# Backward loops of a gated delta-rule layer: one half's decay moves from VectorE's three-plane product to ScalarE and GpSimd

## The chip, the cores and the metric

The kernel runs on one core of a Trainium2 chip. The metric is the device time of one execution in microseconds (us), inputs in device memory to outputs in device memory. Before the change three runs took 650.96, 650.63 and 649.58 us; the median is 650.63 us.

## The reference

The model is one layer over x of shape (4, 1024, 128): a layer norm, a linear attention with a recurrent state, a residual, a second layer norm, and a mixture of 16 experts with a shared expert, again with a residual. The loops that the change touches belong to the attention. With 16 heads of width 8 its state S is an 8x8 matrix for each head and batch, and one step is

```
bs1 = einsum('bhk,bhkv->bhv', kt, S);   S1 = S + at[..., :, None] * bs1[..., None, :]
S2  = exp(gft)[..., None] * S1
bs2 = einsum('bhk,bhkv->bhv', kt, S2)
S3  = S2 + at[..., :, None] * bs2[..., None, :] + kt[..., :, None] * vt[..., None, :]
o   = einsum('bhk,bhkv->bhv', qt, S3)
out3 = stack([z, z, o], axis=2).reshape(B, 3 * N, H, HD);   out = out3[:, -N:]
```

Only the last third of the steps reaches the output, but their state depends on all 1024 steps.

## The kernel before

The 1024 tokens of each batch are cut into 32 chunks, which lie side by side in the 128 columns (4 batches x 32 chunks) while the 128 partitions hold heads and key rows. The first region of each chunk has L1 = 21 positions, the second L2 = 11, so there are NT = 32 positions. Since a step is linear in S, every chunk's whole effect can be computed before its start state is known. That is done by the backward loops: they start at the last position of a region, carry for each chunk an 8x8 matrix (rows that are multiplied into the steps from the left), and take 32 steps, 21 for the first region and 11 for the second. Later the chunks are chained (65 small products in series), then 11 forward steps run from the true start states, and the experts' part runs beside and behind them.

In the backward loops the carried state has 128 x 1024 values, in two halves of 512 columns, half 1 and half 0. Half h lies in PSUM bank 2h. Step n (n = 0 to 31 in all that follows, numbered by the `u_term` with which VectorE begins it) does for each half:

- `u_term` (L1490, VectorE): multiplies the sums over a head's rows, which TensorE left in bank 2h+1, by the factors PP, into SBUF.
- `y_term` (L1496, VectorE): multiplies the sums in bank 2h by the keys K, in place.
- `add_u_term` (L1091, GpSimd): adds the u term to the decayed state (`decayed`, which is plane 0 of `grown`).
- `move_on` (L1502, VectorE): adds `decayed` to bank 2h, which gives the next state, in the same bank.
- `grow` (L1468, VectorE): multiplies the new state by three planes of factors in one instruction, FF (the decay), Y and K. Planes 1 and 2 (`work`) feed TensorE, plane 0 is `decayed`. It is issued by `step`, for half 1 before the `move_on` of half 0, and for half 0 behind it.
- `sums` (L1878 and L1879, TensorE): two products with a block matrix over `work`, two passes each, into banks 2h+1 and 2h.
- beside this, ScalarE copies bank 2h+1 to SBUF (L883), GpSimd multiplies the copy by the values V (`v_times_u`, L1008), and TensorE adds the result to a running sum (`add_sum`, L1888).

Every engine works through its own queue in the order in which the code was written; semaphores hold an instruction until what it needs is there. Nothing reorders them. Between these steps lies the front work of later positions, four positions to a group: a table (`uses`) says at which step TensorE transposes and projects the group, ScalarE evicts the projections from PSUM (L733, L740, L746), and VectorE (`keys` L1405, `c_keys` L1412, `rk_of` L1396) and GpSimd (`gate_keys` L1047, `y_of` L1054, `y_keys` L1063, `p_of` L1069) finish its factors. The group for step n+3 gets its keys, values and queries at steps 2, 6, 10, 14, 18 and 22, its gates and decays one step later. PSUM banks 6 and 7 are handed round for all this (`port`, `taken`): TensorE waits for the eviction of a bank before it fills it again.

## Time and profile before

| | |
|---|---|
| median of three runs | 650.63 us (649.58 to 650.96) |
| the profiled execution | 648.87 us, its span 647.1 us |
| PE busy | 516.5 us, 80% |
| VectorE (DVE) busy | 489.2 us, 76% |
| GpSimd (POOL) busy | 363.1 us, 56% |
| ScalarE (ACT) busy | 257.0 us, 40% |
| backward loops | from 24 us to 308 us |

The profile lists what each engine did and when. The chain that ended last follows the end of the program back through whatever released each instruction. In it "issue" is time in which an engine waited for nothing visible. In the rows of the time line the first number is the start and the second the duration, both in us; a bracket at a row's end is the idle time of the engine before it and what ended that. PE rows are matrix products, and their ends are modelled. The shares of busy time are averages over very different stages; only the backward loops matter here.

### The profile page before, as it was taken

What the parts mean: (1) busy time and instruction counts of PE and PEld (TensorE: products, weight loads), DVE (VectorE), ACT (ScalarE), POOL (GpSimd) and SP (SyncE); (2) the same over time, 40 slices, a digit from 0 to 9 for tenths busy, and PEclk for the clock granted to TensorE, in tenths of its full rate; (3) what the DMA queues carried; (4) which work ended last, traced back from release to release, by engine and by line L of the source; (5) the groups of instructions that cost most, each with busy time, mean ns of one, the idle gap of its engine ahead of it and who ended that gap; (6) DMA issues with size and microseconds to landing.
All of it is one profiled execution on the core that took longest, in us unless ns stands there. A gap on an engine that the chain in (4) does not pass through costs nothing.

```text
span 647.1 us, 7400 instructions
## 1 busy us (share of the span) xinstructions
PE 516.5 (80%) x1809; PEld 269.2 (42%) x1810; DVE 489.2 (76%) x787; ACT 257.0 (40%) x542; POOL 363.1 (56%) x353
## 2 busy tenths in 40 slices
PE   3889899999999885777776889789999956398830
PEld 2543434444444332322444455434443353355520
DVE  5697999989898998999799997788999656322201
ACT  4477543444444432112442345524554115044510
POOL 2378776757576564764786343567766574600033
PEclk9999999999999999988999899989999968889985
DMA  7701138400000691000711133101100011112134
GB/s 179 191 18 32 33 89 217 113 1 1 1 1 1 171 344 38 1 0 0 187 43 41 42 97 73 50 9 32 32 16 9 13 54 32 53 50 65 57 85 114
DMA packets 46946, 41.79 MB, mean 65 GB/s; under 512 B 4700, under 2 KB 40360, under 8 KB 46536
## 3 DMA queue, kind: packets, MB, share of 16 engines
q1 hardware_dynamic: 43332, 35.61, 20.2%
q0 software_dynamic: 2448, 5.38, 3.0%
q10 hardware_dynamic: 1136, 0.46, 0.3%
q8 instruction: 12, 0.20, 0.1%
q14 instruction: 18, 0.15, 0.1%
HBM read 23.80 MB, written 17.63 MB: 64 GB/s over the span
## 4 chain that ended last, share of the span: by engine, by line
PE 35%; DVE 29%; issue 14%; POOL 12%; DMA 4%; ACT 3%; SPq 0%; POOLq 0%; DVEq 0%; ACTq 0%
PE ps L1925 10%; DVE grown L1468 9%; PE ps L1942 5%; POOL grown L1091 4%; DVE ps L1502 4%; PE ps L1878 3%; PE ps L1932 2%; DVE early L1569 2%; DVE grown L1490 2%; PE ps L1982 2%; PE ps L1683 2%; POOL uv L1008 2%; PE ps L1879 2%; POOL early L1037 2%; PE ps L1983 2%
## 5 line engine op out<-in xcount | busy, mean ns | idle before, releaser
L1091 POOL TENSOR_TENSOR grown<-grown 128x512 f32<-128x512 f32 x64 | 80.5, 1267 | 91.6 <-DVE grown L1490 91.6
L1468 DVE TENSOR_TENSOR grown<-ps,steps 128x1536 f32<-128x1536 f32 x64 | 112.1, 1752 | 1.6
L1878 PE MATMUL ps<-grown,cst 128*128 128x512 f32 x128 | 72.7, 650 | 25.3 <-DVE grown L1468 24.7
L883 ACT ACTIVATE uv<-ps 128x512 f32<-128x512 f32 x64 | 38.1, 597 | 104.8 <-DVE grown L1490 104.8
L1925 PE MATMUL ps<-steps 128*128 x128 | 68.8, 635 | 8.4 <-issue 8.2
L1008 POOL TENSOR_TENSOR uv<-uv,steps 128x512 f32<-128x512 f32 x64 | 67.4, 1075 | 1.9 <-ACT uv L883 1.9
L1879 PE MATMUL ps<-grown,cst 128*128 128x512 f32 x128 | 67.1, 606 | 0.0
L1360 DVE TENSOR_TENSOR e_h<-rk,ps 128x256 f32<-128x256 f32 x64 | 25.4, 418 | 53.4 <-ACT rk L900 34.6
L1888 PE MATMUL ps<-uv,cst 128*128 128x512 f32 x128 | 60.4, 594 | 0.6 <-POOL uv L1008 0.6
L1167 POOL TENSOR_TENSOR early<-state,qT 128x512 f32 x22 | 37.1, 1688 | 34.0 <-DVE state L1482 34.0
L1490 DVE TENSOR_TENSOR grown<-ps,steps 128x512 f32<-128x512 f32 x64 | 43.3, 676 | 7.4 <-PE ps L1878 7.4
L1502 DVE TENSOR_TENSOR ps<-ps,grown 128x512 f32<-128x512 f32 x60 | 41.6, 693 | 9.4 <-POOL grown L1091 9.4
L1037 POOL DMA_INDIRECT early<-ys_mixed,slots_mixed x11 | 10.5, 956 | 64.7 <-DMA ys_mixed<-e_y 61.7
L1496 DVE TENSOR_TENSOR ps<-ps,steps 128x512 f32<-128x512 f32 x64 | 44.1, 689 | 1.1 <-PE ps L1879 1.0
L1878 PEld LDWEIGHTS ps<-grown,cst 128*128 128x128 f32 x128 | 21.0, 196 | 57.2 <-DVE grown L1468 51.2
L1138 POOL COPY early<-early 128x32 f32<-128x32 f32 x63 | 27.2, 434 | 28.1 <-DVE early L1574 28.0
L1569 DVE TENSOR_TENSOR early<-early 128x256 f32<-128x256 f32 x63 | 40.1, 636 | 1.3
L900 ACT ACTIVATE rk<-ps 128x256 f32<-128x256 f32 x64 | 23.9, 383 | 39.9 <-PE ps L1925 38.2
L1879 PEld LDWEIGHTS ps<-grown,cst 128*128 128x128 f32 x128 | 25.2, 197 | 32.2 <-issue 32.2
L1942 PE MATMUL ps<-steps,e_hT 128*128 x256 | 35.9, 284 | 2.8 <-ACT e_hT L904 2.7
L1888 PEld LDWEIGHTS ps<-uv,cst 128*128 128x128 f32 x128 | 24.2, 190 | 31.8 <-issue 29.6
L1942 PEld LDWEIGHTS ps<-steps,e_hT 128*128 128x128 f32 x256 | 31.5, 191 | 9.1 <-issue 8.0
(228 smaller groups left out, 1008.0 us busy)
## 6 DMA issues: line engine op xcount, KB each, us to landing
steps<-gate_up_proj SPq DMA_DIRECT2D x1, 4096.0 KB, 16.7
xs_others<-zeros SPq DMA_DIRECT2D x1, 2496.0 KB, 11.0
steps<-xs_others SPq DMA_DIRECT2D x19, 128.0 KB, 2.2
ys_others<-e_y SPq DMA_DIRECT2D x19, 128.0 KB, 1.8
early<-chain_m SPq DMA_DIRECT2D x4, 512.0 KB, 6.3
xf<-x SPq DMA_DIRECT2D x4, 495.0 KB
normed<-early SPq DMA_DIRECT2D x28, 64.0 KB, 1.7
xs_mixed<-zeros SPq DMA_DIRECT2D x1, 1728.0 KB, 8.9
```

Source lines behind the costliest of these rows:

```text
L1008: return G.tensor_tensor(wide(dst, w), wide(src, w), per_col(tile, k, 1, h, w), ALU.mult)
L1091: G.tensor_tensor(decayed[:, h], decayed[:, h], work[:, h, 1], ALU.add).then_inc(s_add[h], 1)
L1468: V.tensor_tensor(grown[:, :, h].rearrange("p e (x w) -> p e x w", w=HD), st, per_col(tile, FF, 3, h, HD), ALU.mult).then_inc(s_prod[h], 1)
L1490: V.tensor_tensor(wide(work[:, h, 1], HD), wide(ps[h][:, 1], HD), per_col(tile_of(i), PP, 1, h, HD), ALU.mult).then_inc(s_uterm[h], 1)
L1496: V.tensor_tensor(wide(bank[2 * h], HD), wide(bank[2 * h], HD), per_col(tile_of(i), K, 1, h, HD), ALU.mult).then_inc(s_term[h], 1)
L1502: V.tensor_tensor(dst, bank[2 * h], decayed[:, h], ALU.add).then_inc(s_state[h], 1)
L1569: V.tensor_tensor(ch_pr[:, m % 2, :, :, 0:HD], ch_m[r][:, :, i, :].rearrange("p j i -> p i j").unsqueeze(1) .to_broadcast([P, 4, HD, HD]), ...
L1878: T.matmul(bank[2 * h + 1], c["block"], work[:, h, 1], start=True, stop=True).then_inc(s_usum[h], 1)
L1879: T.matmul(bank[2 * h], c["minus"], work[:, h, 0], start=True, stop=True).then_inc(s_red[h], 1)
L1888: T.matmul(bank[4 + h], c["ident"], vterm[:, h], start=i in (0, L1), stop=i + 1 in (L1, NT)).then_inc(s_ba[h], 1)
L1925: T.matmul(b_gu(run, b)[u], e_xT[:, b, u], gu[:, bass.ds(ex * (2 * F), 2 * F)], start=True, stop=True).then_inc(s_eg, 1)
L1942: ins = T.matmul(b_y(run)[:, u * D:(u + 1) * D], e_hT[:, u, f * P:(f + 1) * P], dw[:, bass.ds(ex[u] * F + f * D, D)], start=(f == 0), stop ...
```

## The change

In half 1 the decay plane leaves VectorE's product. `grow(1, ...)` now writes two planes (Y and K, 128x1024), while `grow(0, ...)` still writes three. ScalarE copies bank 2, the state of half 1, to a new SBUF buffer `rows_copy`, behind its two `uv` copies and ahead of its front work, and GpSimd multiplies this copy by FF into `decayed` in a new `decay_rows`, behind the u term's addition of half 0. Two semaphores are new. `s_rc` says that the copy is made; both GpSimd and the VectorE's `grow(1)` wait for it, the latter since TensorE may overwrite bank 2 once `grow` has ended. `s_rd` says that GpSimd has made the product; the next copy and the next addition wait for it. At step 0 the state is a constant and no copy is made: `decay_rows(0)` reads the constant.

```diff
             for i in range(NT):
 ...
                     S.activation(ucopy[:, h], bank[2 * h + 1], ACT.Copy).then_inc(s_uc[h], 1)
+                if i + 1 < NT:
+                    act.wait_ge(s_state[1], i + 2 + (i + 1 >= L1))
+                    act.wait_ge(s_rd, i + 1)
+                    S.activation(rcopy[:], bank[2], ACT.Copy).then_inc(s_rc, 1)
                 front(i)
...
+            def decay_rows(step):
+
+                if step:
+                    pool.wait_ge(s_rc, step)
+                rows = (rcopy[:].rearrange("p (e x w) -> p e x w", e=1, w=HD) if step else
+                        c["diag8"].unsqueeze(1).unsqueeze(1).to_broadcast([P, 1, P // 2, HD]))
+                G.tensor_tensor(wide(decayed[:, 1], HD), rows, per_col(tile_of(step), FF, 1, 1, HD), ALU.mult
+                                ).then_inc(s_rd, 1)
+
+            decay_rows(0)
             for i in range(1, NT + 1):
                 coming = NEED.index(i + 2) if i + 2 in NEED[2:] else None
+                pool.wait_ge(s_rd, i)
                 add_u_term(1, i - 1)
...
                 add_u_term(0, i - 1)
+                if i < NT:
+                    decay_rows(i)
                 if coming is not None:
                     y_of(coming)
...
-            def grow(h, tile, ready):
+            def grow(h, tile, ready, copied):
 
+                lo = 1 if h else 0
                 dve.wait_ge(s_state[h], ready)
-                st = bank[2 * h].unsqueeze(1).to_broadcast([P, 3, HALF]).rearrange("p e (x w) -> p e x w", w=HD)
-                V.tensor_tensor(grown[:, :, h].rearrange("p e (x w) -> p e x w", w=HD), st, per_col(tile, FF, 3, h, HD),
-                                ALU.mult).then_inc(s_prod[h], 1)
+                if h and copied:
+                    dve.wait_ge(s_rc, copied)
+                st = bank[2 * h].unsqueeze(1).to_broadcast([P, 3 - lo, HALF]).rearrange("p e (x w) -> p e x w", w=HD)
+                V.tensor_tensor(grown[:, lo:, h].rearrange("p e (x w) -> p e x w", w=HD), st,
+                                per_col(tile, FF + lo, 3 - lo, h, HD), ALU.mult).then_inc(s_prod[h], 1)
```

ScalarE's queue at step 6, where it evicts keys and values of a group (L740 and L746; after the change L742 and L748). First as it was, with the two `uv` copies ahead:

```order
L883 ACTIVATE uv<-ps 128x512 [waits s_bp1,s_uterm1]
L883 ACTIVATE uv<-ps 128x512 [waits s_bp0,s_uterm0]
L740 ACT_TABLE_LOAD
L740 ACTIVATE steps<-ps 128x4x128 [waits s_filled7]
L746 ACTIVATE steps<-steps 128x4x128 [waits s_taken7]
```

The same place in ScalarE's queue after the change:

```order
L885 ACTIVATE uv<-ps 128x512 [waits s_bp1,s_uterm1]
L885 ACTIVATE uv<-ps 128x512 [waits s_bp0,s_uterm0]
L889 ACTIVATE rows_copy<-ps 128x512 [waits s_rows_decayed,s_state1]
L742 ACT_TABLE_LOAD
L742 ACTIVATE steps<-ps 128x4x128 [waits s_filled7]
L748 ACTIVATE steps<-steps 128x4x128 [waits s_taken7]
```

The table load and all evictions of the step now stand behind a copy that waits for half 1's next state.

GpSimd's queue at the same step 6 and the start of step 7, before the change (L1091 the additions, L1047, L1054 and L1063 the group's factors, L1008 the products with V):

```order
L1091 TENSOR_TENSOR grown<-grown 128x512 [waits s_uterm1]
L1047 TENSOR_TENSOR steps<-steps 128x4x128 [waits s_taken6]
L1091 TENSOR_TENSOR grown<-grown 128x512 [waits s_uterm0]
L1054 TENSOR_TENSOR steps<-steps 128x4x128 [waits s_taken7,s_gk]
L1008 TENSOR_TENSOR uv<-uv,steps 128x512 [waits s_ba1,s_uc1]
L1008 TENSOR_TENSOR uv<-uv,steps 128x512 [waits s_ba0,s_uc0]
L1063 TENSOR_TENSOR e_y<-steps 128x512 [waits s_filled6,s_y]
L1091 TENSOR_TENSOR grown<-grown 128x512 [waits s_uterm1]
```

And after it:

```order
L1097 TENSOR_TENSOR grown<-grown 128x512 [waits s_uterm1,s_rows_decayed]
L1053 TENSOR_TENSOR steps<-steps 128x4x128 [waits s_taken6]
L1097 TENSOR_TENSOR grown<-grown 128x512 [waits s_uterm0]
L1105 TENSOR_TENSOR grown<-rows_copy,steps 128x512 [waits s_rows_copied]
L1060 TENSOR_TENSOR steps<-steps 128x4x128 [waits s_taken7,s_gk]
L1014 TENSOR_TENSOR uv<-uv,steps 128x512 [waits s_ba1,s_uc1]
L1014 TENSOR_TENSOR uv<-uv,steps 128x512 [waits s_ba0,s_uc0]
L1069 TENSOR_TENSOR e_y<-steps 128x512 [waits s_filled6,s_y]
L1097 TENSOR_TENSOR grown<-grown 128x512 [waits s_uterm1,s_rows_decayed]
```

One product (L1105) is new, and everything behind it up to the next step's addition is one product later in the queue.

VectorE's queue from the `y_term` of half 0 to the `grow` of half 0, before:

```order
L1496 TENSOR_TENSOR ps<-ps,steps 128x512 [waits s_red0]
L1468 TENSOR_TENSOR grown<-ps,steps 128x3x512 [waits s_state1]
L1502 TENSOR_TENSOR ps<-ps,grown 128x512 [waits s_add0,s_term0]
L1468 TENSOR_TENSOR grown<-ps,steps 128x3x512 [waits s_state0]
L1405 TENSOR_TENSOR steps<-steps,ps 128x4x128 [waits s_filled6]
```

And after:

```order
L1518 TENSOR_TENSOR ps<-ps,steps 128x512 [waits s_red0]
L1490 TENSOR_TENSOR grown<-ps,steps 128x2x512 [waits s_rows_copied,s_state1]
L1524 TENSOR_TENSOR ps<-ps,grown 128x512 [waits s_add0,s_term0]
L1490 TENSOR_TENSOR grown<-ps,steps 128x3x512 [waits s_state0]
L1424 TENSOR_TENSOR steps<-steps,ps 128x4x128 [waits s_filled6]
```

The order is the same. Half 1's `grow` has one plane less and one wait more.

## Rows read from the trace of the kernel before

**Rows 1.** The page's costliest groups: busy us, mean ns, idle before and its releaser.

```profile
L1468 DVE TENSOR_TENSOR grown<-ps,steps 128x1536 f32<-128x1536 f32 x64 | 112.1, 1752 | 1.6
...
L883 ACT ACTIVATE uv<-ps 128x512 f32<-128x512 f32 x64 | 38.1, 597 | 104.8 <-DVE grown L1490 104.8
```

**Rows 2.** Windows of steps 5 and 6: length, then busy PE, PEld, DVE, ACT, POOL.

```profile
76.27:84.21 7.94, 6.92 (x25) 3.54 (x24) 7.65 (x11) 3.48 (x7) 4.56 (x4) 1.00 0.08 20
84.21:91.61 7.40, 6.94 (x16) 2.58 (x14) 7.11 (x9) 4.19 (x6) 6.64 (x6) 1.00 0.33 84
```

**Rows 3.** Time line of step 6 (start us, duration us, engine, line).

```profile
84.21 0.68 DVE L1490 TENSOR_TENSOR grown<-ps,steps 128x512 f32<-128x512 f32 x1
...
84.93 0.60 ACT L883 ACTIVATE uv<-ps 128x512 f32<-128x512 f32 x1 [3.29 <-DVE grown L1490]
84.97 1.27 POOL L1091 TENSOR_TENSOR grown<-grown 128x512 f32<-128x512 f32 x1 [3.44 <-DVE grown L1490]
...
86.34 0.70 DVE L1502 TENSOR_TENSOR ps<-ps,grown 128x512 f32<-128x512 f32 x1 [0.25 <-POOL grown L1091]
...
87.55 1.75 DVE L1468 TENSOR_TENSOR grown<-ps,steps 128x1536 f32<-128x1536 f32 x1
...
89.88 2.10 POOL L1008 TENSOR_TENSOR uv<-uv,steps 128x512 f32<-128x512 f32 x2
```

**Rows 4.** A two-plane product of the forward steps, queried by its line.

```profile
L1461 DVE TENSOR_TENSOR grown<-state,steps x22: 1224/1226/2122, 406.0 to 500.6; 128x1024 f32<-128x1024 f32 x22
```

**Rows 5.** Time line of step 7 (91.61 to 100.40).

```profile
93.17 2.49 POOL L1091 TENSOR_TENSOR grown<-grown 128x512 f32<-128x512 f32 x2
...
94.53 0.70 DVE L1502 TENSOR_TENSOR ps<-ps,grown 128x512 f32<-128x512 f32 x1 [0.93 <-POOL grown L1091]
```

**Rows 6.** Time line of step 14 (150.74 to 158.79).

```profile
153.26 1.28 ACT L740 ACT_TABLE_LOAD   x1
...
154.88 0.60 ACT L740 ACTIVATE steps<-ps 128x512 f32<-128x512 f32 x1 [0.33 <-PE ps L1683]
...
156.77 1.04 PE L1746 MATMUL ps<-wT,wnat 128*128 128x16 f32 x8
157.65 1.10 PE L1878 MATMUL ps<-grown,cst 128*128 128x512 f32 x2
```

**Rows 7.** Time line of step 3 (58.10 to 68.11): evictions, and TensorE behind them.

```profile
62.24 0.70 DVE L1502 TENSOR_TENSOR ps<-ps,grown 128x512 f32<-128x512 f32 x1 [2.15 <-POOL grown L1091]
...
62.83 0.60 ACT L740 ACTIVATE steps<-ps 128x512 f32<-128x512 f32 x1 [0.81 <-PE ps L1683]
63.54 0.30 PEld L1705 LDWEIGHTS ps<-e_y,cst 128*128 128x128 f32 x2 [0.72 <-issue]
...
64.82 0.23 PE L1714 MATMUL ps<-cst,wnat 16*128 16x16 f32 x1
```

**Rows 8.** Time line of step 1 (41.11 to 50.69): an eviction, and its end.

```profile
45.16 0.60 ACT L740 ACTIVATE steps<-ps 128x512 f32<-128x512 f32 x1 [0.29 <-PE ps L1683]
...
50.01 0.31 ACT L717 ACTIVATE rstd<-mv,eps 128x11 f32<-128x11 f32 x1
50.34 0.23 DVE L1375 RECIPROCAL rstd<-rstd 128x11 f32<-128x11 f32 x1 [1.21 <-ACT rstd L717]
```

**Rows 9.** Time line of step 21, the first of the second region.

```profile
215.85 1.75 DVE L1468 TENSOR_TENSOR grown<-ps,steps 128x1536 f32<-128x1536 f32 x1
...
216.67 1.08 ACT L883 ACTIVATE uv<-ps 128x512 f32<-128x512 f32 x2
```

**Rows 10.** Time line of step 22: a table load and what follows.

```profile
223.80 1.28 ACT L740 ACT_TABLE_LOAD   x1
225.09 0.49 ACT L740 ACTIVATE steps<-ps 128x384 f32<-128x384 f32 x1
```

**Rows 11.** The chain at the end of the loops: start us, us, what.

```profile
307.23 0.70 DVE state L1502
307.95 2.91 DMA chain_m<-state
```

More of the change, by code:

```diff
@@ L287, in build @@
         s_usum, s_uterm = two("s_usum"), two("s_uterm")
+        s_rc, s_rd = sem("s_rows_copied"), sem("s_rows_decayed")
         s_bc = sem("s_bcopy")
@@ L375, in build @@
         e_h, e_hT = sb("e_h", [P, U, F]), sb("e_hT", [P, U, F])
+        rcopy = sb("rows_copy", [P, HALF])
         xnT = [e_h[:].rearrange("p u f -> p (u f)"), e_hT[:].rearrange("p u f -> p (u f)")]
@@ L1519, in step @@
                     dve.wait_ge(s_yk, NEED.index(i) + 1)
-                grow(h, tile_of(i), i + 1 + (i >= L1))
+                grow(h, tile_of(i), i + 1 + (i >= L1), i)
             step(1, 0)
```

## The prediction

> **What bounds the kernel now.** I first read the chain that ended last. Its end of the backward loops shows the last `move_on` and, 0.02 us behind it, the transfer of the result [rows 11]. So the loops lie on the path, and whatever they gain or lose goes one to one into the total. Then the costliest groups: the three-plane `grow` is VectorE's largest there, 1752 ns, 64 times, with only 1.6 us idle before all of them [rows 1]. The windows of single steps say who sets the pace. In step 5 VectorE is busy for 7.65 of 7.94 us and GpSimd for 4.56. In step 6, where GpSimd also makes a group's factors, VectorE has 7.11 of 7.40 us and GpSimd already 6.64 [rows 2]. VectorE bounds, but GpSimd has 3.4 us to spare in the one and 0.8 us in the other, and the change adds a product of about 1.05 us to each. Last I read single steps on the time line, to see where ScalarE, TensorE and GpSimd stand ready and where VectorE waits for them.
>
> **What is removed.** The reader should see in step 6 that `grow` for half 1 takes 1.75 us [rows 3]. No row shows two planes from PSUM; two planes from SBUF take 1.23 us (1226 ns) [rows 4]. The bounds are 0.69 us, about what one plane takes (0.68 to 0.70 in rows 3), and 1.75. I take 1.23, the nearest row, which also lies half way between one plane and three. Saved: 0.52 us in each of 32 products. The first, ahead of step 0, gains nothing, I expect, since what follows it there waits for TensorE; 31 remain.
>
> **What the new wait costs.** The chain of the copy runs: half 1's `move_on`, the copy on ScalarE, `grow`. In step 6 the `move_on` starts at 86.34 and ends at 87.04 [rows 3]. ScalarE picks up a VectorE result after 0.04 us (84.21 + 0.68, then the copy at 84.93) [rows 3], copies 128x512 from PSUM in 0.60 us (597 ns) [rows 1], so the copy ends at 87.68. The handoff to VectorE has two bounds: 0.02 us (50.01 + 0.31 to 50.34, an instruction with one wait) [rows 8] and 0.10 us (84.97 + 1.27 to 86.34, with two) [rows 3]. `grow` has two waits now, so I take 0.10: it starts at 87.78 instead of 87.55, 0.23 us later. Half 0's `y_term`, a one-plane product like those of rows 3, runs meanwhile and hides the rest of the copy. Net per step: 0.52 − 0.23 = 0.29 us gained. Behind the waiting `grow` stand half 0's `move_on` and `grow`, and TensorE waits for both.
>
> The Trainium skill (VectorE: DVE Perf Modes, Rules for kernel authors) advises to take an elementwise operation on a matrix product from PSUM as it is, or to copy it to SBUF first if many operations follow. Here one follows. By that rule the change should not pay, and the rows above agree as far as they go: 0.74 us of copy and handoffs to move a plane worth 0.52 us. What saves the sum from the whole 0.74 is the `y_term` beside it.
>
> **Where the gain arrives whole.** 17 steps: 0, 4, 5, 8, 9, 12, 13, 16, 17, 20 and 24 to 30. There GpSimd has room for 1.05 us more, and ScalarE's front work is late by less than TensorE or VectorE need: 17 x 0.29 = 4.9 us gained.
>
> **GpSimd's full steps.** In steps 2, 6, 10, 14, 18 and 22 the new product stands ahead of `y_of`, both `v_times_u` and `y_keys`, and the next step's first addition is behind them all. It costs 1.05 us (two products with V in 2.10 us) [rows 3]; bounded below by nothing, were GpSimd idle, and above by 1.27, the price of its other operations [rows 3]. In step 7 the addition already comes late: it starts at 93.17, 1.56 us into the step, where in step 6 it started 0.76 in, and VectorE stood idle 0.93 us for it, until 94.53 [rows 5, 3]. There is no slack left, so half 1's `move_on` of step 7 comes 1.05 us later, and steps 6 and 7 gain only step 7's 0.29 against it: +0.76. The same in 10 and 11: together +1.5 us. Steps 22 and 23, whose VectorE queue is longer, absorb most: −0.3.
>
> **ScalarE's late evictions.** The table load and the evictions of the group now stand behind the copy, which ends 3.47 us into a step. In step 14 the table load began at 153.26, 2.52 us into it, and the keys' eviction at 154.88, 4.14 in, held up only by TensorE [rows 6]. Now the load ends at 3.49 + 1.28 = 4.77 and the eviction starts at 4.79, 0.65 later. TensorE needs the freed banks for the queries and the logits (156.77) before it can start on `sums` (157.65) [rows 6], and in this step it is TensorE that VectorE waits for. So the whole 0.65 is lost and no gain is seen; a little of GpSimd's lateness comes on top: +0.7 for steps 14 and 15, +0.7 for 18 and 19. Step 1 ends with a table load and a square root for which VectorE waits (50.01, 50.34), behind an eviction at 45.16 [rows 8]; copy and table load bring that eviction to 45.85: +0.7. In step 3 the `move_on` at 62.24 [rows 7] comes 1.05 later (GpSimd also zeroes memory in step 2), the copy ends at 64.64, the table load at 65.95, and the gates' eviction starts at 65.97 instead of 62.83. TensorE needs 1.5 us from there (63.54 to 64.82 + 0.23) [rows 7] before `sums`, which puts these at about 68.2 and the next step at 69.3, where it was 68.11: +1.2 for steps 2 and 3.
>
> By the Trainium skill (ScalarE: Activation LUTs, What ACT_TABLE_LOAD costs) a switch takes some 2.66 us, a load of 1283 ns and a drain of 1380. The load is 1.28 us here, but the drain is not seen: at step 22 the load ends at 225.08 and the next instruction starts at 225.09 [rows 10]. By the rule evictions behind the late load would slip by another 1.4 us; the row decides against it.
>
> **Step 21.** ScalarE makes an extra copy of the running sums, and its two `uv` copies end at 217.75, where `grow` had started at 215.85 [rows 9]. The copy of half 1 starts behind them, ends near 218.25, and `grow` starts at 218.35, 2.5 us later: +2.0 with its saving.
>
> **Sum.** −4.9 + 1.5 − 0.3 + 1.4 + 0.7 + 1.2 + 2.0 = +1.6 us. The profiled execution took 648.87 us for its span of 647.1; it would take 650.5. The median of the runs shown is 1.76 us above it: 650.63 + 1.6 = 652.2 us. No change is what lies within 0.2%, or 1.3 us, about what a measurement of this kernel can tell; the forecast lies just beyond it on the slow side.
>
> **Rivals.**
> Faster, the queues absorb it. The places are the full steps of GpSimd and ScalarE. If half of what I charge there (6.8 us without the −0.3, over seven places) were hidden, as ScalarE's 257 us of busy time and GpSimd's 6.64 of 7.40 us would allow if a little earlier work moved into the gaps, the sum would be 1.6 − 3.4 = −1.8: 648.8 us; if all were hidden, 31 x 0.29 = 9.0 us gained, 641.6. It decides for faster from 2.9 us hidden. Against it: each queue is fixed, and VectorE's idle 0.93 us in step 7 shows that the slack there is spent. Chance 0.22.
> No change, the handoff is short. If VectorE picks the copy up after 0.02 instead of 0.10 us, 31 steps give 2.5 us back: 652.2 − 2.5 = 649.7; half of it gives 651.0. For it speaks the row with one wait, against it the one with two. Chance 0.29.
> Slower by more, the copy itself comes late. If ScalarE were still in its front work when the `move_on` ends, every such step would stall VectorE. At 0.3 us in each of 14 steps with front work: 652.2 + 4.2 = 656.4. Against it: ScalarE's idle time before its copies is 104.8 us in 64 of them [rows 1]. Chance 0.09.
> The forecast itself has 0.40.
>
> **Numbers.** Faster 0.22, within 0.2% 0.29, slower 0.40 + 0.09 = 0.49. The handoff gives −2.5 us, a product of 1.27 us on GpSimd +0.7 over three pairs, a second wait resolved only after the first another +0.04 x 31 = +1.2. With part of either rival beyond that the range is 647.0 to 656.5 us; the forecast's own is 650.0 to 654.5.
>
> **What would show it.** The two-plane product at 1.23 us; half 1's `grow` 1.44 us behind the start of its `move_on`, with an idle time before it put down to ScalarE's copy; plain steps shorter by 0.29 (step 5: 7.65 instead of 7.94); step 6 at 7.1 but step 7 at 9.8 instead of 8.79; step 14 longer, 8.7 instead of 8.05; step 21 at 10.8 us. Steps 7 and 14 unchanged in length would refute the costs and make it faster; an idle time at every `grow` much over 0.1 us would make it slower than I say.

## The result: 9.1 us slower, where 1.6 us were forecast

The changed kernel takes 659.51 us (median of 4 runs, 656.54 to 661.14) where the kernel before takes 650.41 beside it: 1.0136 times as long, 95% interval 1.0097 to 1.0175. Repeated twice it gave 1.0154 (1.0111 to 1.0197) and 1.0153 (1.0125 to 1.0181). The forecast was 652.2 and its range ended at 656.5. The sign was right and most single prices were, but the sum was short by 7.5 us. Three steps of the forecast failed: the term of 4.9 us for the steps in which "the gain arrives whole" (1.7 us arrived in the trace), the sentence that what the loops lose "goes one to one into the total" (4.7 to 6.3 us more were lost behind them), and TensorE's clock, which was put at nothing without a reason. The section on why the prediction was right and wrong takes them one by one.

The absolute time of a kernel moves from set to set of runs (the kernel before had medians of 650.4, 657.9, 650.6, 657.6 and 650.5 us, two of them on one chip at different times), so only kernels of one set are compared below.

The page of the changed kernel, its costliest groups (busy us, mean ns, idle before and its releaser), to be held against [rows 1]:

```profile
L1097 POOL TENSOR_TENSOR grown<-grown 128x512 f32<-128x512 f32 x64 | 80.5, 1268 | 59.8 <-DVE grown L1512 59.8
L1490 DVE TENSOR_TENSOR grown<-ps,steps 128x1024 f32<-128x1024 f32 x64 | 95.4, 1491 | 8.2 <-ACT rows_copy L889 3.6
...
L1524 DVE TENSOR_TENSOR ps<-ps,grown 128x512 f32<-128x512 f32 x60 | 41.6, 694 | 13.4 <-POOL grown L1097 13.4
...
L1105 POOL TENSOR_TENSOR grown<-rows_copy,steps 128x512 f32<-128x512 f32 x31 | 33.3, 1075 | 6.5 <-ACT rows_copy L889 6.5
```

`grown` costs VectorE 95.4 us instead of 112.1: the 16.7 us are gone. GpSimd got 33.3 us of work for it, and VectorE's idle time before `grown` rose from 1.6 to 8.2 us.

Steps 5 and 6 of the changed kernel in windows (length, then busy PE, PEld, DVE, ACT, POOL), which answer to [rows 2] (the three numbers at the end are TensorE's granted clock, the busy share of the DMA engines and GB/s):

```profile
77.66:85.37 7.71, 6.78 (x25) 3.40 (x24) 7.22 (x11) 4.08 (x8) 5.64 (x5) 1.00 0.16 42
85.37:92.54 7.17, 6.90 (x16) 2.58 (x14) 6.68 (x9) 4.79 (x7) 6.34 (x6) 1.00 0.32 85
```

Both steps are shorter by 0.23 us (7.94 and 7.40 before). The mechanism of the forecast is there, at 0.23 instead of 0.29. The time line of the changed kernel's steps 6 and 7, all engines, shows where the difference went (start us, duration us, engine, line):

```profile
85.37 0.68 DVE L1512 TENSOR_TENSOR grown<-ps,steps 128x512 f32<-128x512 f32 x1
...
86.20 1.27 POOL L1097 TENSOR_TENSOR grown<-grown 128x512 f32<-128x512 f32 x1 [1.84 <-DVE grown L1512]
...
87.57 0.70 DVE L1524 TENSOR_TENSOR ps<-ps,grown 128x512 f32<-128x512 f32 x1 [0.32 <-POOL grown L1097]
...
88.30 0.60 ACT L889 ACTIVATE rows_copy<-ps 128x512 f32<-128x512 f32 x1 [0.42 <-DVE ps L1524]
...
89.00 1.22 DVE L1490 TENSOR_TENSOR grown<-ps,steps 128x1024 f32<-128x1024 f32 x1
...
89.88 1.08 POOL L1105 TENSOR_TENSOR grown<-rows_copy,steps 128x512 f32<-128x512 f32 x1
...
92.14 2.11 POOL L1014 TENSOR_TENSOR uv<-uv,steps 128x512 f32<-128x512 f32 x2
...
95.43 2.49 POOL L1097 TENSOR_TENSOR grown<-grown 128x512 f32<-128x512 f32 x2
...
96.80 0.70 DVE L1524 TENSOR_TENSOR ps<-ps,grown 128x512 f32<-128x512 f32 x1 [2.26 <-POOL grown L1097]
```

The two-plane product takes 1.22 us and starts 1.43 us behind its `move_on`, both as forecast. But GpSimd starts its addition 0.83 us into step 6, not 0.76 as in [rows 3], because that instruction now has a second wait (which of the two is coded last matters, as shown below). VectorE's `move_on` waits for it and comes 2.20 us in instead of 2.13. Step 7 shows the price of GpSimd's product: VectorE idle for 2.26 us, 0.93 before [rows 5].

### The profile page after: what moved, and what is told of

It is laid out like the page before. It is cut to its first block, busy times and chain, and to the rows that moved or that the text cites. A ratio compares the mean times of both kernels' runs of the same rounds, so it can differ in the third digit from the quotient of the medians.

```text
span 658.4 us, 7549 instructions
## 1 busy us (share of the span) xinstructions
PE 524.1 (80%) x1809; PEld 274.9 (42%) x1810; DVE 479.4 (73%) x787; ACT 274.3 (42%) x573; POOL 395.5 (60%) x385
## 4 chain that ended last, share of the span: by engine, by line
PE 33%; DVE 25%; POOL 14%; issue 14%; ACT 6%; DMA 4%; POOLq 0%; DVEq 0%; SPq 0%; ACTq 0%
PE ps L1947 9%; DVE grown L1490 6%; POOL grown L1097 5%; PE ps L1964 5%; DVE ps L1524 4%; PE ps L1900 3%; ACT rows_copy L889 2%; PE ps L1954 2%; DVE grown L1512 2%; PE ps L1901 2%; DVE early L1591 2%; DVE grown L1480 2%; POOL uv L1014 2%; POOL xs_mixed L1027 1%; POOL early L1043 1%
## 5 line engine op out<-in xcount | busy, mean ns | idle before, releaser
L1490 DVE TENSOR_TENSOR grown<-ps,steps 128x1024 f32<-128x1024 f32 x64 | 95.4, 1491 | 8.2 <-ACT rows_copy L889 3.6
L1900 PE MATMUL ps<-grown,cst 128*128 128x512 f32 x128 | 75.6, 675 | 20.1 <-DVE grown L1490 19.8
L1901 PE MATMUL ps<-grown,cst 128*128 128x512 f32 x128 | 70.8, 637 | 0.0
L1186 POOL TENSOR_TENSOR early<-state,qT 128x512 f32 x22 | 35.1, 1594 | 37.9 <-DVE state L1504 37.9
L1043 POOL DMA_INDIRECT early<-ys_mixed,slots_mixed x11 | 10.5, 956 | 65.0 <-DMA ys_mixed<-e_y 62.0
L1900 PEld LDWEIGHTS ps<-grown,cst 128*128 128x128 f32 x128 | 23.2, 208 | 50.5 <-DVE grown L1490 40.1
L1901 PEld LDWEIGHTS ps<-grown,cst 128*128 128x128 f32 x128 | 26.5, 207 | 34.8 <-issue 34.8
L1910 PEld LDWEIGHTS ps<-uv,cst 128*128 128x128 f32 x128 | 24.2, 190 | 31.9 <-issue 29.9
L1105 POOL TENSOR_TENSOR grown<-rows_copy,steps 128x512 f32<-128x512 f32 x31 | 33.3, 1075 | 6.5 <-ACT rows_copy L889 6.5
```

Of the source, the lines that this page charges most:

```text
L1490: V.tensor_tensor(grown[:, lo:, h].rearrange("p e (x w) -> p e x w", w=HD), st, per_col(tile, FF + lo, 3 - lo, h, HD), ALU.mult).then_inc( ...
L1900: T.matmul(bank[2 * h + 1], c["block"], work[:, h, 1], start=True, stop=True).then_inc(s_usum[h], 1)
L1901: T.matmul(bank[2 * h], c["minus"], work[:, h, 0], start=True, stop=True).then_inc(s_red[h], 1)
L1910: T.matmul(bank[4 + h], c["ident"], vterm[:, h], start=i in (0, L1), stop=i + 1 in (L1, NT)).then_inc(s_ba[h], 1)
```

## Where the time went

The kernel before and the changed one were traced once more, on one chip, beside each other (650.44 and 660.89 us, close to their medians of 650.45 and 660.03). First the kernel before, in two windows: the loops (step 0 to step 31) and all that lies behind them.

```profile
31.71:303.46 271.75, 236.60 (x670) 108.24 (x669) 247.10 (x307) 113.99 (x189) 179.73 (x156) 0.97 0.22 63
303.46:648.60 345.14, 263.96 (x1081) 150.54 (x1079) 222.69 (x396) 128.35 (x324) 173.31 (x182) 0.91 0.20 54
```

The same two windows of the changed kernel:

```profile
31.53:309.28 277.75, 236.56 (x669) 109.91 (x668) 236.11 (x306) 131.48 (x220) 212.81 (x187) 0.96 0.22 62
309.28:659.10 349.82, 266.97 (x1083) 152.24 (x1081) 224.79 (x396) 128.39 (x324) 171.85 (x182) 0.90 0.19 53
```

The loops are 6.0 us longer, although VectorE has 11.0 us less to do in them. The part behind the loops, in which no line was edited, is 4.7 us longer (6.3 in the first pair of traces, 343.65 and 349.93). I had not looked for anything there: my text said that what the loops gain or lose "goes one to one into the total". The third column from the right, TensorE's granted clock, falls by 0.01 in both windows. VectorE's busy time behind the loops rises from 222.69 to 224.79 us for the same 396 instructions, and that led to the cause of 2.0 us.

A forward step behind the loops, in the kernel before: VectorE's two-plane product and GpSimd's product, both released by the same `state`.

```profile
488.05 1.23 DVE L1461 TENSOR_TENSOR grown<-state,steps 128x1024 f32<-128x1024 f32 x1 [0.17 <-DVE state L1482]
488.10 2.13 POOL L1167 TENSOR_TENSOR early<-state,qT 128x512 f32 x1 [0.89 <-DVE state L1482]
```

The same step and the next one in the changed kernel:

```profile
495.54 1.09 POOL L1186 TENSOR_TENSOR early<-state,qT 128x512 f32 x1 [0.90 <-DVE state L1504]
495.84 1.87 DVE L1480 TENSOR_TENSOR grown<-state,steps 128x1024 f32<-128x1024 f32 x1 [0.52 <-DVE state L1504]
...
505.24 1.11 POOL L1186 TENSOR_TENSOR early<-state,qT 128x512 f32 x1 [0.61 <-DVE state L1504]
...
505.29 2.13 DVE L1480 TENSOR_TENSOR grown<-state,steps 128x1024 f32<-128x1024 f32 x1 [0.28 <-DVE state L1504]
```

Whoever starts first takes its own time (1.23 or 1.09 us), the other 0.64 to 1.04 us more. Before, VectorE wins by 0.05 us. Here it starts later (0.52 and 0.28 us behind the state, not 0.17) and loses both: 0.35 + 0.64 and 0.11 + 0.90 us, 2.0 in all. This place is named "the race" below. The Trainium skill (SBUF — State Buffer, Who interferes with whom) says that a VectorE instruction with two inputs in SBUF contends with a GpSimd instruction that reads SBUF, and that issue order decides who blocks; the four rows agree.

## Experiments

**The three parts by themselves** (one set, the kernel before 657.93 us). First VectorE's saving alone:

```diff
-                    S.activation(rcopy[:], bank[2], ACT.Copy).then_inc(s_rc, 1)
...
-                if i < NT:
-                    decay_rows(i)
...
-                if h and copied:
-                    dve.wait_ge(s_rc, copied)
...
-                pool.wait_ge(s_rd, i)
+                pool.wait_ge(s_rd, 1)
```

> The changed kernel without the copy, without GpSimd's products of the later steps and without the waits for them: VectorE's half-1 product has two planes, the decay of half 1 is left out of the computation (its plane keeps what step 0 put there). Theory A (local costs add up step by step, TensorE's lower granted clock beside them is a coincidence of these runs): 31 steps x 0.52 us, less some 3 us in steps 3, 10, 14 and 18 where TensorE sets the pace: about 13 us faster than before, 637 us, and the part behind the loops as long as before to 1 us. Theory B (whatever makes the loops denser lowers TensorE's granted clock, and that costs 5 us or more in and behind the loops): 642 us or more, granted clock at or under 0.935.

This kernel leaves out half 1's decay behind step 0, so it computes something else and only its time counts. 649.61 us, 0.9866 (0.9823 to 0.9908), 8.3 us less, where 13 were expected. Plain steps gain 0.46 (step 5: 7.48), which is 0.52 less the 0.07 of GpSimd's second wait; the pairs with a group's matrices gain less (6 and 7 together 0.47), which fits the waits for GpSimd and TensorE in [rows 5] and [rows 6].

Then the copy alone, with its wait, beside the three-plane product:

```diff
+                if i + 1 < NT:
+                    act.wait_ge(s_state[1], i + 2 + (i + 1 >= L1))
+                    S.activation(rcopy[:], bank[2], ACT.Copy).then_inc(s_rc, 1)
...
+                if h and copied:
+                    dve.wait_ge(s_rc, copied)
```

> The kernel before with ScalarE's copy and VectorE's wait for it alone: half 1's product keeps three planes, nothing uses the copy, GpSimd is as before. Theory A: the wait 0.23 us in 31 steps (7.1 us), late evictions 0.7 us each in steps 1, 14 and 18, step 21 another 2.3 us: about 11.5 us slower, 662 us. Theory B: these 11.5 us and the later stages longer too, 666 us or more, clock under 0.935.

668.60 us, 1.0158 (1.0115 to 1.0201), 10.7 us more. Step 5 takes 8.18 instead of 7.94, step 14 8.70 instead of 8.06, step 21 11.27 instead of 8.76.

And a product of one plane on GpSimd at the place of the new one, from a tile that nothing else writes:

```diff
+                if i < NT:
+                    pool.wait_ge(s_rz, i)
+                    spare_product(i - 1)
```

> The kernel before with one product more per step on GpSimd, at the place of the change's product, over a constant buffer and without a new wait that could bind; nobody uses its result. Theory A: 1.05 us in each of the pairs 2/3, 6/7, 10/11, 0.3 to 0.7 in 14/15, 18/19 and 22/23, and 0.2 us where VectorE's scaling of rk falls beside it: 4.5 to 6 us slower, 655 to 656.5 us. Theory B (clock): 660 us or more. If GpSimd's queue still had room, no change: 650.4.

664.36 us, 1.0093 (1.0064 to 1.0123), 6.4 us more. Step 5 is unchanged (7.95); steps 3, 7, 15 and 19 are longer by 1.00 to 1.04 us, 11 by 2.06 and 12 by 0.68. The three differences add up to −8.3 + 10.7 + 6.4 = +8.8 us, against +9.1 to +10.0 for the whole change. Each is known to 2 or 3 us only, so a meeting worth a few us would not be seen in the sum. TensorE's clock does show one: its mean over the runs is 0.9338, 0.9345 and 0.9345 in the three parts and 0.9341 in the kernel before, so none lowers it by itself, while the next kernel of the same set, which has all three, has 0.924 (0.922 to 0.926).

```diff
-                pool.wait_ge(s_rd, i)
-                add_u_term(1, i - 1)
+                add_u_term(1, i - 1, i)     # waits for s_uterm, then for s_rd
...
-                dve.wait_ge(s_state[h], ready)
                 if h and copied:
                     dve.wait_ge(s_rc, copied)
+                dve.wait_ge(s_state[h], ready)
```

> The changed kernel with the order of waits turned round in two places: VectorE's half-1 product waits first for the copy and then for the state, GpSimd's addition first for the u term and then for the product, so that the signal that comes last is the one that the instruction itself waits for. Theory A with two handoffs of 0.07 us too long in 31 steps each: 3 to 4 us faster than the change, about 655.5 us. If only the number of waits counts and not their order: as the change, 659.5 us.

664.64 us in the set of 657.93, 1.0101 (1.0056 to 1.0145). Rows of GpSimd, VectorE and ScalarE in its step 6, which starts at 86.17:

```profile
86.93 1.27 POOL L1099 TENSOR_TENSOR grown<-grown 128x512 f32<-128x512 f32 x1 [1.71 <-DVE grown L1513]
...
88.30 0.70 DVE L1525 TENSOR_TENSOR ps<-ps,grown 128x512 f32<-128x512 f32 x1 [0.25 <-POOL grown L1099]
...
89.03 0.60 ACT L889 ACTIVATE rows_copy<-ps 128x512 f32<-128x512 f32 x1 [0.36 <-DVE ps L1525]
...
89.67 1.23 DVE L1491 TENSOR_TENSOR grown<-ps,steps 128x1024 f32<-128x1024 f32 x1
```

The addition starts 0.76 us in again, and `grown` follows the copy after 0.04 us instead of 0.10. Step 6 takes 7.04 instead of 7.17, step 5 7.58 instead of 7.71: 0.13 less each, half of it GpSimd's wait. The number of waits is what it was; only the place of the late one differs. The changed kernel wasn't in this set, so its total is no measure of the 0.13; it is 6.7 us above the kernel before, where some 5 to 6 were expected.

The same in `next_state` of the kernel before (first `s_add`, then `s_term`), in the set of 650.56 us:

```diff
-                dve.wait_ge(s_term[h], i + 1)
                 dve.wait_ge(s_add[h], i + 1)
+                dve.wait_ge(s_term[h], i + 1)
```

> The kernel before with one exchange: the addition that gives the next state waits first for GpSimd's sum and then for VectorE's own term. Theory A (the signal that comes last should be the first wait in the code: then one handoff of 0.10 us becomes 0.03): 0.06 us in each of some 25 steps, 1.5 us faster, ratio 0.998. If order does not matter: 1.000.

648.99 us, 0.9990 (0.9968 to 1.0012): not told from no change. The trace has the 0.07 us in single steps (step 5 at 7.87, step 6 at 7.33).

**The pair again**, in that set:

> The kernel before, unchanged, timed against itself on the chip where the others of this group run. Both theories: a ratio of 1.000. What it tells is the spread and the trace of before on this chip. Theory A' (the part of the change's time behind the loops, some 6 us, is the granted clock of the chip and of the moment, not the change): its steps 0 to 31 take 270.9 us as in the first trace but for half-rate stretches, while the part behind step 31 may differ from the first trace's 343.6 us by several us, with nothing changed. Theory B (the change lengthens that part): that part stays at 343.6 to 1 us.

> The changed kernel, unchanged, timed against before on the same chip. Theory A' (local costs of some 4 us in the loops at full clock, and the parts of VectorE alone, copy and wait, product, which measured -8.3, +10.7 and +6.4 us, add up): +8.8 us by the parts, +4 us by the steps at full clock; so a ratio of 1.006 to 1.013. Theory B (clock is lowered by the change): 1.015 or more here, where the clock is low from the start, or the same 1.014 with a part behind step 31 that is longer than before_again's by 5 us.

649.23 us, 0.9986 (0.9965 to 1.0008), and 660.56 us, 1.0154. The mean granted clock over the runs is 0.9409 for the kernel before and 0.9325 for the changed one (0.9397 and 0.9317 in the set of 650.50): the change lowers it. One place where: step 3 took 11.42 us in the first trace of the changed kernel and 13.01 in this one. Two of TensorE's rows in the time line of this trace, then the windows of the hole between them and of what follows:

```profile
62.51 1.02 PE L1705 MATMUL ps<-e_hT,wfo 128*128 128x512 f32 x2
66.47 1.74 PE L1727 MATMUL ps<-e_y,cst 128*128 128x512 f32 x2 [2.94 <-ACT steps L742]
```

```profile
63.53:66.40 2.87, 0.00 (x1) 0.00 (x0) 2.70 (x5) 2.55 (x4) 2.58 (x3) 1.00 0.01 3
66.80:70.20 3.40, 3.40 (x7) 1.47 (x6) 2.03 (x2) 1.32 (x5) 2.04 (x2) 0.50 0.00 0
```

TensorE stands idle for 2.9 us, waiting for the gates' eviction that the copy and the table load have pushed back; then its granted clock is 0.50 (1.2 of 2.4 GHz) for 3.4 us, and step 3 loses another 1.6 us. The hole alone does not decide it: in the first trace it is as long (2.95 us, until 66.88) and no half-rate time follows it; there a stretch had fallen into step 1, at 38.5 to 41.9 us. The half-rate time inside the loops is 9.8, 10.2 and 13.7 us in three traces of the kernel before and 24.2, 20.9 and 20.9 in three of the changed one.

**The product moved only where there is room**, with the waits in the better order, in the same set of 650.56 us:

```diff
+        MOVED = [1, 5, 6, 9, 10, 13, 14, 17, 18, 21, 25, 26, 27, 28, 29, 30, 31]
+        moved = lambda i: sum(m <= i for m in MOVED)
...
-                if i + 1 < NT:
+                if i + 1 in MOVED:
...
-                lo = 1 if h else 0
+                lo = 1 if h and copied in [0] + MOVED else 0
...
             def next_state(h, i, dst):
+                dve.wait_ge(s_add[h], i + 1)
                 dve.wait_ge(s_term[h], i + 1)
-                dve.wait_ge(s_add[h], i + 1)
```

> The change only in the 17 steps where by the step table it gains (steps 0, 4, 5, 8, 9, 12, 13, 16, 17, 20 and 24 to 30); in the others VectorE keeps its three planes and there is no copy and no product. The waits are in the order that wait_order showed to be quicker, in the two places of the change and in the addition that gives the next state. Theory A: 0.35 us in each of 17 steps, less 0.2 in the five with rk, and some 0.06 in each addition: 6 us faster than before, ratio 0.991. If the gain per step is lost whenever GpSimd has more to do at all: 1.000 or above.

644.79 us (643.38 to 645.46), 0.9918 (0.9889 to 0.9947): 5.8 us faster than the kernel before. Not all of it is the moved product: the exchange in `next_state`, measured above by itself, is in this kernel too. With it alone the kernel before took 648.99 us in the same set; against it the gain is 4.2 us, and the two intervals (0.9889 to 0.9947, 0.9968 to 1.0012) don't meet. Its loops and two of its steps, in windows:

```profile
32.33:298.09 265.76, 234.13 (x670) 107.67 (x669) 242.05 (x307) 123.78 (x206) 197.88 (x173) 0.98 0.23 65
...
75.67:83.17 7.50, 6.57 (x24) 3.36 (x23) 7.21 (x11) 4.01 (x8) 5.63 (x5) 1.00 0.13 33
...
99.30:107.44 8.14, 7.01 (x26) 3.80 (x25) 7.70 (x12) 3.89 (x6) 6.82 (x6) 1.00 0.83 224
```

Step 5 gains 0.44 us, 0.07 of it by the exchange (7.87 with the exchange alone), and the full steps are left as they were (step 7: 8.80). Step 8 gains 0.03 only, and against the exchange alone (8.09) it loses 0.05, as step 4 does (8.14, 8.10): by these figures two of the 17 steps would be better left out. This is the place of the maximum on `rk`. In the kernel before it follows `grown` while GpSimd is through:

```profile
104.83 2.12 POOL L1008 TENSOR_TENSOR uv<-uv,steps 128x512 f32<-128x512 f32 x2
...
107.88 0.18 DVE L1396 TENSOR_SCALAR rk<-rk 128x64 f32<-128x64 f32 x1
```

In the changed kernel GpSimd's two products end a microsecond later in the step, at 110.00:

```profile
107.90 2.10 POOL L1014 TENSOR_TENSOR uv<-uv,steps 128x512 f32<-128x512 f32 x2
...
109.64 0.42 DVE L1415 TENSOR_SCALAR rk<-rk 128x64 f32<-128x64 f32 x1
```

The maximum takes 0.42 instead of 0.18 us and ends 0.06 us behind GpSimd's product. Tested by leaving it out (set of 657.59 us):

```diff
-                V.tensor_scalar(ap, ap, NORM_EPS, None, ALU.max).then_inc(s_nm, 1)
-                dve.wait_ge(s_nm, n + 1)
```

> room_only without VectorE's maximum of the key norms with 1e-12 (L1415 of the changed kernel), which changes no value that occurs; only its reciprocal is left. If that maximum, an operation from SBUF to SBUF with one tensor input, stands still while GpSimd's last product runs (it took 0.32 to 0.42 us in steps 4, 8 and 12 of the changed kernel and 0.18 before, and ended 0.05 us behind GpSimd each time), steps 4, 8, 12, 16 and 24 lose 0.22 us for the instruction and another 0.15 to 0.25 for the waiting: step 8 7.7 us instead of 8.14. If the reciprocal is held up in the same way, only some 0.2 us. Total: 2 us faster than room_only at most.

652.48 us, 0.9937 (0.9916 to 0.9958), no more of a gain than that of the kernel with the maximum in its own set (0.9918). The steps do show it: 4 and 8 take 7.55 instead of 8.14 us, 12 and 16 7.80 instead of 8.14. That is 0.34 to 0.59 us for an instruction of 0.18, so what it waits for, with the handoff behind it, is worth 0.16 to 0.41. The trace shows where the total may have been lost: half-rate stretches fell into steps 1 (11.48 instead of 9.58) and 26 (10.02 instead of 9.13).

**Full steps of GpSimd without late gates**: copy and product also in steps 2, 6, 10 and 22, and still not in 3, 7 and 11, where the copy would stand ahead of the gates' eviction.

```diff
-        MOVED = [1, 5, 6, 9, 10, 13, 14, 17, 18, 21, 25, 26, 27, 28, 29, 30, 31]
+        MOVED = [1, 3, 5, 6, 7, 9, 10, 11, 13, 14, 17, 18, 21, 23, 25, 26, 27, 28, 29, 30, 31]
```

> As room_only (same order of waits), with the plane moved also in steps 2, 6, 10 and 22; left with VectorE are the steps 1, 3, 7, 11, 14, 15, 18, 19, 21 and 23, in which ScalarE's evictions would come late behind the copy. GpSimd's four full steps carry the new product. Theory C (the change costs granted clock because ScalarE's late evictions leave TensorE idle for 2 to 3 us, and TensorE's rate falls to half behind such a hole; the time behind the loops grows with it): no hole, so the clock as before, 0.940, and the local sum alone: room_only's 5.8 us less 0.7 us in each of three pairs: 4 us faster than before, ratio 0.994. Theory D (GpSimd's lateness is what costs the clock, since VectorE and TensorE then both wait): clock 0.935, ratio 1.000 or more.

656.62 us in the set of 657.59, 0.9997 (0.9977 to 1.0016): the whole gain is gone, where a ratio of 0.994 was expected. Against the kernel with the product only where there is room the pairs cost 1.04 us (steps 2 and 3), 1.03 (6 and 7) and 1.11 (10 and 11), which is one product each, and 22 and 23 0.22. Another 1.5 went in step 12, at half rate. The clock is not lower than that of the kernel before in this set (0.9347 and 0.9354 over the runs), though its trace has that stretch. So what the moved work does to the clock is not read cleanly from this kernel, and of the two theories that it was to tell apart neither is confirmed.

**Is it only that everything is later?** An idle stretch of writes ahead of the loops in the kernel before, 3 of them and 15 of them:

```diff
+            for k in range(3):          # range(15) in the long one
+                if k:
+                    dve.wait_ge(s_idle, k)
+                V.memset(idle[:], 0.0).then_inc(s_idle, 1)
```

> The kernel before with three small memsets of an unused buffer on VectorE ahead of its first statistics, so that everything behind them comes some 1.5 us later. If the part behind step 31 is longer after the change only because it starts at another moment of the gate's own rhythm, this part should move by several us here as well, either way. If not: the whole is 1.5 us later and that part stays at 343.5 us to 1 us.

> The same with fifteen memsets, about 7 us, as late as the changed kernel is at the end of its loops. If being later is what lengthens the part behind step 31, it takes 349.5 us here as in the changed kernel and the total is 13 us longer; if not, 343.5 us and 7 us longer, the clock as before.

660.09 us, 1.0037 (1.0017 to 1.0056), and 669.13 us, 1.0172 (1.0152 to 1.0193), in the set of 657.59. Step 0 starts 2.2 and 10.6 us later than in the second trace of the kernel before, and the totals are 2.5 and 11.5 us up. By the medians lateness alone costs itself and at most 0.9 us more (2.1 at the end of the long one's interval), so it does not explain the unedited part being 4.7 to 6.3 us longer. The traces are less even: 352.7 and 356.1 us behind the loops, the second in the slowest of that kernel's four runs, and the kernel before was not traced in this set.

**The race.** In the traces so far the two VectorE products of the last two forward steps had lost it in exactly the kernels in which all 31 steps wait for the copy (the changed one, its repeat, the one with the other order, the copy alone) and in none of the others. What these four share, and no other has, is 23 more instructions of VectorE ahead of that place, which is a loop of two turns in VectorE's program. (The number is my count of the program's instructions; waits are not in the traces.) Two kernels to tell position from moment, with the pair beside them (set of 650.50 us):

> The kernel before, traced on the same chip as the three beside it. Expected 0 against itself. Behind the last step of the loops the part without any edit took 343.5 and 343.7 us in two traces of before, and 349.7 and 349.9 in two of the changed kernel; this trace gives the reference for the others. In that part 3 of 22 two-plane products of the forward steps lost the start to GpSimd's product from the state in before, and 5 in the changed kernel; here I expect that the two of the last two forward steps start first and take 1.23 us.

> The changed kernel once more, beside before on the same chip. Expected +9 to +10 us (1.014 to 1.015). Theory of the position: in the last two forward steps GpSimd's product starts first, VectorE's takes 1.87 and 2.13 us instead of 1.23, and this is 2.0 us of the part behind the loops. Theory of the clock: the rest of the 6 us there is half-rate time of TensorE, more than in before on the same chip.

650.45 us, 1.0007 (0.9989 to 1.0025), and 660.03 us, 1.0153 (1.0125 to 1.0181). The products are at 1.23 us in the first and at 1.87 and 2.13 in the second.

The kernel before with 23 idle instructions in front of the forward steps (47 waits in the code, 23 instructions more by the same count):

```diff
+            for k in range(47):
+                dve.wait_ge(s_xf, 16 * 3 * B)
             dve.wait_ge(s_chout, 32)
```

> The kernel before with 23 more instructions in VectorE's program, all of them waits that are long met, between its last work ahead of the forward steps and the forward steps. This puts the loop of the last two forward steps at the place that it has in the changed kernel (instruction 848 of VectorE's instead of 825). If the position decides, the two products lose the start and take 1.87 and 2.13 us: +2.0 us, and up to 1 us for the waits themselves, 1.003 to 1.005. If not, they take 1.23 us and the time is 0 to +1 us.

Its time line at the place, GpSimd's and VectorE's rows:

```profile
488.07 1.09 POOL L1167 TENSOR_TENSOR early<-state,qT 128x512 f32 x1 [0.89 <-DVE state L1482]
488.38 1.87 DVE L1461 TENSOR_TENSOR grown<-state,steps 128x1024 f32<-128x1024 f32 x1 [0.52 <-DVE state L1482]
...
497.84 2.13 DVE L1461 TENSOR_TENSOR grown<-state,steps 128x1024 f32<-128x1024 f32 x1 [0.28 <-DVE state L1482]
```

To the hundredth the rows of the changed kernel: 0.52 and 1.87, 0.28 and 2.13, in a kernel whose loops are those of before. Between 483 and 500 us it falls back 2.0 us against the first trace of the kernel before. The total does not show it: 650.83 us, 1.0013 (0.9996 to 1.0031, which reaches up to 2.0 us), with less half-rate time in its trace than the kernel before has beside it (73.6 against 76.8 us). Where the half-rate time behind the loops is the same (60.0 us here, 60.3 and 60.2 in the first two traces of the kernel before), the part behind the loops is 345.6 us here and 343.7 and 343.5 there. These 2.0 and 2.1 us agree with the race, though the idle instructions' own time is in them too.

The changed kernel with the last two forward steps of VectorE written out:

```diff
-                with dve.Fori(RUNS[1].n + 2, L2) as i:
+                for i in range(RUNS[1].n + 2, L2):
                     step(i, False)
```

> The changed kernel with the last two forward steps of VectorE's program written out one after the other instead of in a loop of two turns; the work is the same. If VectorE is late there because of the jump into that loop and back, at the place in its program to which 23 more instructions ahead have moved it, then both products start first again and take 1.23 us, and the kernel is 2.0 us faster than the changed one beside it (+7 to +8 us against before). If the race is decided by something else (the moment, GpSimd, a transfer), they stay at 1.87 and 2.13 and the time stays at +9 to +10.

```profile
494.95 1.22 DVE L1480 TENSOR_TENSOR grown<-state,steps 128x1024 f32<-128x1024 f32 x1
...
495.13 2.00 POOL L1186 TENSOR_TENSOR early<-state,qT 128x512 f32 x1 [0.89 <-DVE state L1504]
```

VectorE starts 0.04 us behind the state and wins again. 657.74 us (656.29 to 658.05), 1.0124 (1.0100 to 1.0149), 2.3 us under the changed kernel beside it; the intervals of the two overlap, so it is the traces that decide: the part behind the loops takes 346.4 us instead of 349.8, of which some 2 are the race, while the loops are at 277.1 and 277.8. The half-rate time there is lower too, 66.5 against 69.9 us.

## Why the prediction was right and wrong, step by step

**What the edits cost where they are** was mostly right. By the first pair of traces:

| steps | forecast us | measured us |
|---|---|---|
| `grow` of two planes | 1.23 | 1.22 to 1.23 |
| `grow` behind its `move_on` | 1.44 | 1.42 to 1.46, but for steps 20 and 21 |
| step 1 | +0.7 | +1.62 (+0.7 without a half-rate stretch) |
| 2 and 3 | +1.2 | +1.19 (+2.8 in the two later traces, by a half-rate stretch) |
| 6, 7, 10 and 11 | +1.5 | +1.59 |
| 14, 15, 18 and 19 | +1.4 | +1.53 |
| 21 | +2.0 | +1.98 |
| 22 and 23 | −0.3 | 0.0 |
| the 17 steps with a whole gain | −4.9 | −1.7 |
| loops in all | +1.6 | +6.2 |

The late gates (forecast: step 14 at 8.7, step 21 at 10.8; measured 8.76 and 10.74) can be read off the changed kernel's time line of ScalarE and VectorE:

```profile
156.50 1.28 ACT L742 ACT_TABLE_LOAD   x1
157.79 0.60 ACT L742 ACTIVATE steps<-ps 128x512 f32<-128x512 f32 x1
...
220.75 0.62 ACT L889 ACTIVATE rows_copy<-ps 128x512 f32<-128x512 f32 x1
...
221.47 1.22 DVE L1490 TENSOR_TENSOR grown<-ps,steps 128x1024 f32<-128x1024 f32 x1 [2.34 <-ACT rows_copy L889]
```

The eviction starts 4.84 us into step 14 (4.79 forecast, 4.14 in [rows 6]), with the load's end and nothing between: no drain here either. In step 21 `grown` waits 2.34 us for the copy.

**"Where the gain arrives whole" failed**, by 3.2 us, for three reasons. GpSimd's addition got a second wait and starts 0.07 us later in every step; I had charged the second wait of `grow` and put any further second wait into the range only (0.04 us each, 1.2 in all). It cost 0.06 in each of 16 steps, 1.0 us, and the kernel with the waits in the other order has it back. In 4, 8, 12, 16 and 24 VectorE's maximum on `rk` runs into GpSimd's product that is now a microsecond later, and instead of 0.23 us the gain is 0.12 or a loss of 0.03 to 0.05: about 1.0 us. And step 26 met a half-rate stretch (10.08 instead of 9.04): 1.3 us with the gain it should have had. That stretch is not proper to the change: the third trace of the kernel before has 9.89 there. Nor is the one in step 1: the kernel before with three idle writes ahead of it has 10.52 there instead of 9.58.

**The handoff** was in the rivals and went as in the forecast (0.10 us). The rival "the handoff is short" did not come true here, but does once the copy's wait is coded first: 0.04 us.

**TensorE's clock** was in no step of mine. Steps 1 and 26 in the first trace, 3 and 26 in the others lose 0.9 to 1.6 us each. That steps 2 and 3 met their forecast of +1.2 in the first trace is luck in part: no stretch fell there. The stretch in step 3 follows on a hole in TensorE's work that my own term (the late gates) makes; I priced the hole and not what came behind it in two of three traces.

**"One to one into the total" failed** by the largest single piece. In the pair of traces on one chip the total rises by 10.5 us: −0.2 ahead of the loops, +6.0 in them, +4.7 behind them. Of the last, 2.0 us are the race. That it takes this time and that the position of the loop decides it is shown in the traces of two kernels, one for each direction; their totals are too coarse to show 2.0 us. The other 2.7 go with 6.8 us more of half-rate time there (69.9 against 63.1 us). That they come from the clock is argued, not shown: lateness alone doesn't do it by the medians, and no kernel here set the clock by itself. So the cause of the loss behind the loops is open but for the race.

**The rivals.** "The queues absorb it" fell: each full step cost what it was charged. "The copy itself comes late" fell too; it is on time but for step 21.

The range was too narrow above because it was built from the forecast's own terms, each of them within the loops. Every term that was left out is a cost of work that meets other work: an addition behind a second wait, a maximum and a product behind GpSimd's, TensorE's clock behind a hole.

## What to carry to other kernels

Move work to another engine only in the steps where that engine has room: with the waits in the better order the move in all 31 steps costs 6.7 us, and in 17 of them it gains 4.2 to 5.8. Where an instruction waits for two semaphores, code first the one that ends last (seen in single steps, 0.07 us each; the totals are too coarse for it). After any edit compare the busy time of instructions that were not edited: where it differs, two engines have met, even far behind the edit.

## What the hardware showed that I had not expected

- The wait that ends last costs 0.06 to 0.07 us more if it is coded last and not first: 0.10 against 0.04 us for `grow` behind the copy, 0.83 against 0.76 us for GpSimd's addition.
- 23 idle instructions of VectorE ahead of a loop delay its first product in each of two turns by 0.35 and 0.11 us, which is enough to lose a start that was won by 0.05 us, and 2.0 us with it. With the loop written out the delay is gone. So the loop and its position are shown to matter; how they do it is not.
- A maximum over 64 columns takes 0.18 us, or 0.42 while GpSimd multiplies, and ends right behind GpSimd's product. By the Trainium skill (SBUF — State Buffer, Who interferes with whom) such a form of tensor_scalar can use both port pairs of VectorE and is then held off as a whole; the end 0.06 us behind GpSimd's agrees.
- The level of a set of runs, whatever the kernel: 650.5 and 657.9 us for the same kernel on the same chip at different times. In traces of the slower sets TensorE's granted clock is 0.50 for 27 to 34 us on end between 514 and 565 us, for 17 us in the others.
